# The front of the retention: head 0's first scores between the last turns, the last turns in other banks, first high parts ahead of the last copies

## What is computed

```python
x = x + _L0_ffn_ref(_layernorm(x), ...)            # y: gate-weighted outputs of one expert matrix
x = x + _L1_xattn_ref(_layernorm(x), ctx, ctx, Wh, ...)

# _L1_xattn_ref, 4 heads of 128, b = 8, s = 256
Q = einsum('bshd,hde->bshe', xh, Wh); K, V = the same of ctx
scores = einsum('bshe,bthe->bhst', Q, K) / sqrt(hd)
masked = scores * Dn
A = maximum(abs(masked.sum(axis=0)), 1.0)          # summed over the batch
O = einsum('hst,bthe->bshe', A, V)
Y = groupnorm(O) * gamma + beta
out = relu(x @ wg) * Y @ wo
```

## Time and profile before

| | us |
|---|---|
| median of 3 runs | 1123.99 |
| the three runs | 1122.95 to 1124.54 |
| the profiled execution, its time | 1123.79 |
| the profiled execution, its span | 1122.0 |

### The profile page before, as it was taken

The page is one execution under the profiler, slowest core; times in us unless marked ns, Lnnn a source line. Parts: engine busy times, 40 slices in busy tenths (PEclk is TensorE's granted clock), DMA queues, the critical chain, the costliest instruction groups (busy, mean ns, idle before and its releaser), DMA issues.

```text
span 1122.0 us, 13371 instructions
## 1 busy us (share of the span) xinstructions
PE 1062.5 (95%) x4924; PEld 861.9 (77%) x4924; DVE 603.7 (54%) x1040; ACT 447.7 (40%) x801; POOL 608.7 (54%) x438
## 2 busy tenths in 40 slices
PE   5799999578998999999999999999999999999997
PEld 5677777455677988887778888888888888888886
DVE  5399999855884563578442442424424253242223
ACT  4454454342165656645342332233222332322232
POOL 1488997211032466122166776667766776767662
PEclk9899999788998999999999999999999999999999
DMA  9211221000011010005132222433224323232211
GB/s 312 97 56 50 65 57 38 1 1 1 0 38 39 1 39 30 1 1 221 40 115 100 77 71 78 147 148 113 72 104 155 117 108 101 76 108 90 87 55 38
DMA packets 24560, 85.49 MB, mean 76 GB/s; under 512 B 3168, under 2 KB 3824, under 8 KB 23728
## 3 DMA queue, kind: packets, MB, share of 16 engines
q1 hardware_dynamic: 22384, 80.45, 21.1%
q10 hardware_dynamic: 2112, 4.19, 1.0%
HBM read 74.85 MB, written 9.78 MB: 75 GB/s over the span
## 4 chain that ended last, share of the span: by engine, by line
PE 61%; DVE 1%; POOL 1%; issue 1%; ACT 0%; POOLq 0%
PE banks L331 20%; PE banks L332 20%; PE banks L333 20%; PE banks L326 1%; PE banks L1265 0%; POOL wgl L570 0%; DVE stat L1469 0%; PE banks L1274 0%; POOL gul L596 0%; DVE xres L1840 0%; POOL xtr L553 0%; ACT xn L684 0%; DVE xf L1727 0%; PE banks L1330 0%; DVE zf L1880 0%
## 5 line engine op out<-in xcount | busy, mean ns | idle before, releaser
L1851 DVE TENSOR_TENSOR hf<-banks,silu 128x512 f32<-128x512 f32 x132 | 91.3, 692 | 323.5 <-PE banks L333 322.3
L596 POOL TENSOR_TENSOR gul<-wst,guh 128x1280 fp32r<-128x1280 f32 x44 | 129.9, 2951 | 141.7 <-DVE guh L1734 135.8
L606 POOL TENSOR_TENSOR hl<-hf,hh 128x512 fp32r<-128x512 f32 x129 | 178.3, 1413 | 8.6 <-ACT hh L946 8.6
L988 PE MATMUL banks<-kv,strip 128*128 128x288 f32 x640 | 158.3, 411 | 4.1 <-POOL kv L496 4.1
L946 ACT ACTIVATE hh<-hf 128x512 fp32r<-128x512 f32 x132 | 83.6, 633 | 190.4 <-DVE hf L1851 190.4
L988 PEld LDWEIGHTS banks<-kv,strip 128*128 128x128 f32 x640 | 123.3, 193 | 38.8 <-issue 4.3
L944 ACT ACTIVATE silu<-banks 128x512 f32<-128x512 f32 x132 | 78.9, 598 | 167.0 <-PE banks L333 166.9
L331 PE MATMUL banks<-xf,guh 128*128 128x512 f32 x352 | 137.2, 390 | 0.8 <-POOL gul L596 0.8
L332 PE MATMUL banks<-xf,guh 128*128 128x512 f32 x352 | 137.0, 389 | 0.0
L333 PE MATMUL banks<-xf,gul 128*128 128x512 f32 x352 | 136.9, 389 | 0.0
L530 POOL TENSOR_TENSOR rstd<-vare,mhalf 128x2 f32<-128x2 f32 x32 | 26.2, 818 | 177.2 <-DVE vare L1478 177.2
(11 more groups left out here) (281 smaller groups left out, 2261.7 us busy)
## 6 DMA issues: line engine op xcount, KB each, us to landing
wst<-in_chunk_w SPq DMA_DIRECT2D x44, 960.0 KB, 4.8
strip<-toep SPq DMA_DIRECT2D x32, 256.0 KB, 3.1
xres<-in_x ACTq DMA_DIRECT2D x4, 1024.0 KB, 13.2
cin<-in_ctx SPq DMA_DIRECT2D x16, 256.0 KB, 5.1
xf_s<-xf SPq DMA_DIRECT2D x2, 2048.0 KB, 7.5
out<-xres SPq DMA_DIRECT2D x16, 256.0 KB, 2.1
xf<-xf_s SPq DMA_DIRECT2D x8, 512.0 KB, 5.8
mk<-hot_s SPq DMA_DIRECT2D x14, 256.0 KB
```

The source lines that it names most:

```text
L596: pool.tensor_tensor(gul[:, u, :], wst[:, u, 0:GU_W], f(guh[:, u, :]), ALU.subtract).then_inc(gul_ready, 1)
L606: pool.tensor_tensor(hl[:, u, s, :], hf[:, s, :], f(hh[:, u, s, :]), ALU.subtract)\
L988: mm = pe.matmul(dst, strip[:, h % 3, far:far + P], view(kv, h % 3, m * BATCH * PAIRS, [[PAIRS, BATCH], [1, PAIRS]]), start=m == 0, stop=m ...
L1851: dve.tensor_tensor(hf[:, s, :], banks[:, 7, :], silu[:, s % 2, :], ALU.mult).then_inc(mul_done, 1)
```

## The change

The twelve score matmuls of head 0's quarter 0 move on TensorE ahead of turns 14 and 15. The two projections of `start` are written behind the turns of n = 4 and n = 5, which is the same place in the order. Turns 12 to 15 go into banks 6 and 7 (`X_BANK`), since scores add up in banks 4 and 5 from then on: turn 12 waits for all expert outputs to be copied out of 6 and 7, and the first scores wait for the first 12 copies of turned tiles, the last readers of 4 and 5. On ScalarE, evac_m(0, 0) moves ahead of copies 10 and 11, high_x(0, 0) ahead of copies 12 and 13, and evac_m(0, 1) and high_x(0, 1) ahead of copies 14 and 15; high_x waits for 4 and 8 copies where it waited for 16. On VectorE low_x(0, 0) moves ahead of low_m(0, 1). No instruction of work is added or taken away.

```diff
@@ -354,6 +354,9 @@
         IN_SEARCH = 11
         END_D = [(ro_act, 2 * RHEADS), (ro_vec, 2 * RHEADS)]
 
+
+        def X_BANK(t):
+            return (4 if t < 12 else 6) + t % 2
 
         def batches(t):
             return t.rearrange("p (b t) e -> p b t e", t=2)
@@ -720,7 +723,7 @@
                 expert_out(t)
             def keep_turned(t):
                 act.wait_ge(xn_turned, TILES + t + 1)
-                act.activation(turned(xt, t), split(banks[:, 4 + t % 2, :]), ACT.Copy).then_inc(xt_copied, 1)
+                act.activation(turned(xt, t), split(banks[:, X_BANK(t), :]), ACT.Copy).then_inc(xt_copied, 1)
 
             def high(dst, src, used, h, q):
 
@@ -753,15 +756,19 @@
                     apply(TILES // 2 + n)
                     if left:
                         expert_out(left.pop(0))
-                    keep_turned(2 * n)
-                    keep_turned(2 * n + 1)
+                    if n == 5:
+                        evac_m(0, 0)
                     if n == 6:
-                        evac_m(0, 0)
-                    if n == 7:
-                        evac_m(0, 1)
-                act.wait_ge(xt_copied, TILES)
-                high_x(0, 0)
+                        act.wait_ge(xt_copied, 4)
+                        high_x(0, 0)
+                    if n < TILES // 2 - 1:
+                        keep_turned(2 * n)
+                        keep_turned(2 * n + 1)
+                evac_m(0, 1)
+                act.wait_ge(xt_copied, 8)
                 high_x(0, 1)
+                keep_turned(TILES - 2)
+                keep_turned(TILES - 1)
 
             def first(h):
                 high_c(h, 0)
@@ -1105,8 +1112,9 @@
                 pe.wait_ge(xn_ready, TILES + t + 1)
                 if t >= 2:
                     pe.wait_ge(xt_copied, t - 1)
-                turn(pe, 4 + t % 2, split(xn[:, t % GROUP, :]), xn_turned)
-
+                if t == 12:
+                    pe.wait_ge(yw_copied, TILES)
+                turn(pe, X_BANK(t), split(xn[:, t % GROUP, :]), xn_turned)
 
             def project(h, q):
 
@@ -1129,6 +1137,8 @@
                 u = q % 2
                 pe.wait_ge(mtl_ready[u], raised(mtl_ready[u]) + 2 * h + q // 2 + 1)
                 pe.wait_ge(xxl_ready, 4 * h + q + 1)
+                if h == 0 and q == 0:
+                    pe.wait_ge(xt_copied, 12)
                 if q == 0:
                     pe.wait_ge(a_read, raised(a_read) + h)
                     pe.wait_ge(ro_act, raised(ro_act) + 2 * h)
@@ -1144,21 +1154,25 @@
                 mm.then_inc(sc_done[u], 1)
 
             def start():
-                for n in range(TILES // 2):
+                for n in range(TILES // 2 - 1):
                     expert_parts((5, 4, 4, 4, KB * TILES)[n] if n < 5 else 0)
-                    if n == 5:
-                        project(0, 0)
-                    if n == 6:
-                        project(0, 1)
                     turn_c(2 * n)
                     turn_c(2 * n + 1)
+                    if n == 4:
+                        project(0, 0)
+                    if n == 5:
+                        project(0, 1)
+                scores(0, 0)
+                turn_c(TILES - 2)
+                turn_c(TILES - 1)
 
             def first(h):
                 project(h, 0)
                 project(h, 1)
 
             def second(h):
-                scores(h, 0)
+                if h > 0:
+                    scores(h, 0)
                 scores(h, 1)
                 project(h, 2)
                 project(h, 3)
@@ -1659,8 +1673,8 @@
                         gated_sum(2 * n + 2)
                         gated_sum(2 * n + 3)
                 low_m(0, 0)
+                low_x(0, 0)
                 low_m(0, 1)
-                low_x(0, 0)
                 low_x(0, 1)
                 dve.wait_ge(decay_in, 16)
```

## The result

| | before | after |
|---|---|---|
| median, us (nine runs each, side by side) | 1122.95 | 1119.9 |
| lowest to highest | 1119.98 to 1124.54 | 1117.05 to 1120.59 |
| ratio of the runs | | 0.9971, 95% interval 0.9959 to 0.9983 |
| the profiled execution, its time | 1123.79 | 1118.62 |
| the profiled execution, its span | 1122.0 | 1116.8 |

The changed kernel is faster by 0.29%, between 1.9 and 4.6 us, about 3.3; 4.5 had been forecast. The difference of the two profiled spans, 5.2 us, is not the effect of the change: the changed profile was already 1.84 us ahead at project(0, 1), where both kernels have run the same instructions on TensorE (334.94 there, 333.10 here). Ahead of that point the granted clock was at 0.50 for 41.0 us in the one profile and for 37.5 in the other, in both cases ahead of 300 us, and that makes most of the difference.

A forecast was written before the change was run, and what follows sets the result against it. TensorE was taken as the bound, busy 1062.5 of 1122.0 us, its scores held back by ScalarE. Idling 4.50 to 2.4, clock 2.3, turns 0.3, restarts −0.2 give 4.5: 1124.0 − 4.5 = 1119.5, range 1118.2 to 1122.2.

The forecast's parts named there:

- The hole: TensorE's thin stretch, 338 to 349.5 us: 4.5 of idling and 2.3 of lower clock, 6.8 us at most.
- ScalarE's order as the cause: Ahead of the first scores: ScalarE, never free over 0.40 us from 335.75, writes x's first high part only at 342.36.
- The schedule of steps: ScalarE's new order laid out start to start: `vh` at 343.19 instead of 344.44, project(0, 2) at 344.7 instead of 349.18.
- what the banks cost: Turns 12 to 15 in banks 6 and 7: the new waits of turn 12 and of the scores cost nothing.
- The swap on VectorE "matters": low_m(0, 1) and low_x(0, 0): in the old order the first `xxl` would stand behind an evacuation coming at 340.18.
- rival (c): In the front: scores(0, 0) stand behind a late `xxl`, all behind equally late; a delay of 4.5 gives 1124; chance 0.04.
- No fall of the clock in the new front: From 338 to 350 us the granted clock stays at 1.00, despite three idle pieces of 0.7 to 0.9 us.
- An earlier start should arrive at the end nearly whole: Behind the hole: waits after 360 us follow TensorE's own work, so the 4.5 us gain is kept.
- third sign of being wrong: The prediction is wrong if project(0, 2) to the end is not as long as before, 772.8 us.
- rival (d): Slower: clock falls also at 534 to 536 us (2.7) and once more before 580; 3.1 slower, 1126.9; chance 0.04.
- The list of waits: TensorE's waits after 360 us: 2.2 us for `xf` in the feed-forward front and 0.3 once for `ccl`.
- the third fall: Falls in the new front, at 534 to 536 us and once more before 580: 2.2 + 2.7 + 2.7 − 4.5 = 3.1 slower.

The follow-up runs named there:

- e1: The changed kernel again, no edit, against the kernel before: ratio 0.9963; project(0, 1) to project(0, 2) 9.72 us.
- e4: The kernel before with unread matmuls filling TensorE's two idle stretches in the hole: ratio 1.0000; project(0, 1) to project(0, 2) 11.95 us.
- e2: The changed kernel with scores(0, 0) behind turns 14 and 15 again on TensorE: ratio 0.9982 to the kernel before; project(0, 1) to project(0, 2) 9.72 us.
- e7: The changed kernel with ScalarE's copies 14 and 15 moved behind high_c(0, 2) and evac_v(0, 0): ratio 0.9964 to the kernel before; stretch 8.75 us.
- e3: The changed kernel with scores(0, 0) behind turns 14 and 15 and banks 4 and 5 throughout: ratio 1.0018 to the kernel before; stretch 11.90 us.
- e6: The changed kernel with VectorE's low_m(0, 1) ahead of low_x(0, 0) again: ratio 0.9997 to the kernel before; project(0, 1) to project(0, 2) 14.39 us.
- e8: The changed kernel with last pair's xn and copies later on ScalarE, turns 14 and 15 behind project(0, 2): ratio 0.9970; project(0, 1) to project(1, 0) 15.26 us.
- e11: e3 once more for a second profile: project(0, 1) to project(0, 2) 11.90 us; project(0, 2) to the end 776.53 us.
- e9: The changed kernel with six unread matmuls in the feed-forward front's 1.53 us wait: ratio 0.9979 to the kernel before; project(0, 2) to the end 775.07 us.

## Why the prediction was right, and where it was not

The time, 1119.9, lies in the range (1118.2 to 1122.2) and beside the forecast of 1119.5. That the two times lie so close is luck in part. The three runs shown first had a median 1.0 us above that of all nine, and the gain came out smaller than forecast; the two errors cancel. The forecast difference of 4.5 is the fairer measure, against 3.3 measured here and 3.9 from the medians of e1 (1122.04 and 1118.16).

- *The hole*: right. Idling 4.50 and 2.3 of clock; after it 2.39 of idling, where 2.4 was forecast. e4 measured the clock's share by itself as 2.3.
- *ScalarE's order as the cause*: right for the stretch. The schedule of steps was within 0.15 us. e2 shows that the place of the scores, which the prediction treated as part of the gain's mechanism, moves nothing between project(0, 1) and project(0, 2); e7 shows that `vh` was the last link. But the order is not enough: without the new banks (e3) it is worth nothing in the total. The prediction asked only what the banks cost (nothing) and gave them no part in the gain.
- *The swap on VectorE "matters"*: right, e6. With the scores ahead of the turns the whole gain hangs on it. The delay of e6 is the mechanism of rival (c), though with a steeper price: the scores come 3.35 us later (7.18 behind project(0, 1) in place of 3.83) and project(0, 2) 4.67 later. Rival (c) had the one equal to the other; the clock's fall and the longer wait for `vl` (1.72 in place of 0.81) come on top.
- *No fall of the clock in the new front*: right in all profiles of the changed kernel, e2, e7 and e8. With idle stretches of 1.49 and 1.48 us in a row (e3) it falls.
- *"An earlier start should arrive at the end nearly whole"*: this is the step that was mis-sized, and the prediction's own third sign of being wrong came true: the stretch from project(0, 2) to the end is 774.0 and not 772.8. I took the granted clock behind project(0, 2) to be unchanged. It falls once more at the wait of 1.53 us, and costs 1.1 to 1.2 us in each of the two profiles of the changed kernel. This is the first part of rival (d), which I gave 0.04 and priced at 2.7 for a fall of 6.8 us; it lasts 3.4 and costs 1.2 to 1.3.
- *The list of waits*: not read whole. The prediction names 2.2 us for `xf` and 0.3 for `ccl`, and leaves out the longest wait of the list, for `zl`, and one for `gul`:

```profile
PE banks L331 <- DVE zl L1887: 2.8, 1, 2.8
PE banks L331 <- POOL gul L596: 0.8, 1, 0.8
```

  Neither takes back any of the gain by its length (2.8 and 0.9 in the changed kernel), but the one for `zl` is where the clock falls in five of the fourteen profiles.
- *The sign of rival (d)*: its text says that the total turns slower only from the third fall on. By its own prices the second is enough: 2.2 + 2.7 is 4.9, more than the gain of 4.5. Nothing measured hangs on this.

4.5 less 1.2 is 3.3, the measured difference, but the agreement to a tenth is more than the runs can carry: they allow 1.9 to 4.6. From project(0, 1) to the end the kernel before takes 787.0 us in two profiles and 787.8 and 787.9 in the two that lose the clock at the wait for `zl`, the changed one 783.7 and 783.6: a gain of 3.3 to 4.3.

What stays open is why the clock falls at that wait in the one group of kernels and in no profile of the other, though wait and work are equal. In the four profiles of the kernel before, project(0, 2) starts within 0.5 us of the moment at which the granted clock comes back (349.18 and 349.5 in the first), so everything behind it runs at nearly the same distance from a clock event; the changed kernel has no such event. A fall in the front is not what protects the wait: e3, e11 and e6 have one too, get the clock back 1.0, 0.9 and 3.9 us ahead of project(0, 2), and lose it at the later wait. Nor does the fall keep a fixed place at the wait: in the nine profiles that have it, it comes 1.2 to 2.9 us after the wait has begun. The Trainium skill ("TensorE: Matmul & The Clock Gate", Part 1) says that the gate's timing does not start anew with a kernel, and that the moment of a change depends on where the work falls in it. If so, the same wait could keep the clock at one distance and lose it at another. That agrees with what is seen, but no run here varied the distance alone, so it is argued and not shown.

## What to carry to other kernels

When the bounding engine waits at the seam of two stages, lay out the order of the engine that feeds it step by step. Here a dozen start-to-start steps gave the new start to 0.1 us. In that stretch the orders of the feeding engines made the gain, with the banks that let them; moving the scores on the bounding engine itself made nothing of it. Undo each part of such a change by itself: a part that the plan calls free, here the banks, can decide whether anything is left in the total. Price the lower clock behind a gap with the gap, but don't count on a saved microsecond reaching the end whole: a later wait that kept the clock before may lose it now. For effects of a few us compare stretches between equal instructions in several profiles of both kernels. Two spans differ by up to 3.3 us from what happened ahead of the change.

## What the runs showed of the hardware that I had not expected

- Filling a gap with matmuls holds the granted clock (e4: 1.00 through 4 us of filler, scores at 0.12 instead of 0.22 us each), yet the total did not move (ratio 1.0000, 0.9986 to 1.0014): some 1.2 of the 2.3 us went at a later wait, and the rest is within the interval. The filler of e9 won 1.3 us at its own wait, and its profile lost 2.4 at the next long one.
- The same wait of 1.53 us kept the clock at 1.00 in four of four profiles of one order and lost it for 3.4 us in nine of nine of the others that have no filler there.
- The last wait, of 2.77 us, loses the clock in some executions only, of one and the same kernel too (two of the four profiles of the kernel before): from the first chunk product to the end it takes 559.0 (nine profiles), 560.2 to 560.4 (three) or 561.4 (two, e9 and e11), in kernels that are the same there.
- With equal instructions on TensorE up to there, project(0, 1) starts between 332.8 and 336.1 us, 3.3 apart, as much as the effect that was to be measured. Most of that lies in stretches in which the granted clock was at 0.50 in one profile and not in the other.
